# One core, windowed attention and a graph feed-forward: the second stream's output projection with tokens in rows, its bias and residual added in the PSUM bank by TensorE

## Chip, cores and metric

One Trainium2 (trn2) chip, one of its NeuronCores. The metric is the device time of one execution in microseconds (us); smaller is better. Timed executions of the kernel before took 7975.61, 7982.82 and 7992.23 us, median 7982.82.

## What is computed

The input x is 32 images of 32 x 32 tokens with 128 channels. The reference, cut to what matters:

```python
y  = mhsa(windows(layernorm(x)))                      # stream A: 16 windows of 8x8 tokens, 8 heads
ys = roll(unwindows(y), (-4, -4))
ys = mhsa(windows(ys), shift_mask)                    # stream B: the same weights, masked windows
x  = x + roll(unwindows(ys), (4, 4))                  # x2: residual, 1024 tokens x 128 per image
t  = x + ffn(layernorm(x), edge_index)                # graph attention over 524288 + 32768 edges,
                                                      # top 2 of 4 experts, per token
# mhsa: qkv = x @ w_qkv + b_qkv; softmax(q k^T / 4 + mask) @ v; out @ w_o + b_o   (float32)
```

## The kernel before

The kernel has three stages, one after the other: `attention` (both attention passes of all images and, beside them, a sort of the edge keys on VectorE), `edges` (gathers by GpSimd, segment scans, the experts' matmuls) and `combine` (gates, weighted sum, output).

**Order of the attention stage.** Every engine runs its own program over steps n = -2 to 36, each of eight slots j (PAIRS). In a step stream A works on image n (its inputs for n+1 are being made) and stream B on image n-2; from n = 2 to 31 both are active. In each slot TensorE does, in this order (L899 to L918): `scores` of slot j (L849, matmuls L860 and mask matmuls L865), `turn` of slot j-2 (transposes of the exponentials, L879), `weigh` of slot j-3 (L894), then the slot's tasks. VectorE (L1101 to L1125): `less_maximum` (L1096 reduction and L1098 subtraction, both over the PSUM banks of the scores), operations of the sort (L991 to L997), in every second slot `normalised_output` (L1082, L1085), and in fixed slots layer norm statistics (L980) and `residual`. ScalarE: the exponentials (L724), copies of the turned blocks (L731), normalisation (L688), then the evacuation of each task's bank. There is one pair of score banks: `scores` of slot j+1 waits for L1098 of slot j (`s_sub`).

**Tasks and banks.** A task is a name of `SLOT_TASKS` (L356), such as Ap1 (projection of stream A, half 1). Its matmuls go to one of two PSUM banks `misc`, taken strictly in turn over all tasks (L394 to L399); a task waits until the task two places before it has been evacuated (`s_free`). Blocks of sort keys to be transposed (L842, 136 tasks of the steps with both streams) are put behind the slot's tasks and share the two banks. `LAG` says how many steps behind n the image of a task is.

**Stream B's end.** `attended` (L785, ScalarE L613) transposes the attention output to channels in rows and ScalarE writes it with the bias of v into `attT`, 512 tokens per half (two instructions of 128x256). `projected` (L794 to L803) multiplies by `wo`, channels stay in rows: one matmul of 448 and one of 64 columns undo half of the roll. ScalarE adds `b_o` and writes `zrow` (L643, L645). `result` (L805 to L813, tasks CZ0 and CZ1 of slot 6) transposes `zrow` to tokens in rows, four 128x128 blocks per bank. VectorE adds the residual `xres` out of the bank into `x2` (`residual`, L1055 to L1068), signals `s_x2`, and takes the statistics of four tiles in slot 6 and four in slot 7 (L1116 to L1120). SyncE stores x2 (L502); GpSimd turns the statistics into scales (`deviation`, L550); ScalarE normalises x2 in slots 3 and 5 of the next step.

**The sort's plan.** 754 VectorE operations of the sort are spread over the slots by `place_sort` (L184): each slot gets as much as `spare` (L370 to L378) leaves of `SLOT_US` after the slot's other VectorE work. The stage ends when the last sorted part and the last node rows are stored.

## Time and profile before

| | |
|---|---|
| timed executions (3) | 7975.61 / 7982.82 / 7992.23 us |
| the profiled execution | 7985.52 us, span 7983.8 us |
| attention stage | 0 to about 1979 us, a quarter of the span |
| VectorE busy, 585.7 to 1561.7 us | 931.58 of 976.0 us |
| TensorE matmul busy, the same stretch | 907.34 of 976.0 us |
| ScalarE busy, the same stretch | 764.96 of 976.0 us |
| TensorE's granted clock, the same stretch | 1.00 |

A row of instruction groups has the line in the kernel, the engine, the operation, output<-inputs, shapes and count, then the busy time in us and the mean of one in ns, then the idle time before them and what ended it. A float32 matmul appears as two MATMUL records, a float32 transpose or a bf16 matmul as one. A record's duration includes the pipeline's depth; what an instruction costs its engine in a dense stream is the distance between starts.

### The profile page before, as it was taken

Reading aid. Unit: us, or ns where it says so; the run is one execution under the profiler, and the core shown is the slowest. Engines: PE = TensorE matmul, PEld = TensorE weight load, DVE = VectorE, ACT = ScalarE, POOL = GpSimd, SP = SyncE. Lnnn points to the kernel's source line nnn. Section 1 sums busy time; section 2 is a strip of 40 time slices with the busy share of each in tenths; the row PEclk is TensorE's granted clock in tenths of the full one; section 3 lists DMA queues with packets and bytes.
Section 4 is the critical chain, followed back from the end, with each engine's and each line's share of the span. In section 5 each row is a group of like instructions: output and inputs, shape, how many; then the busy total and the mean of one; then the engine's idle time right before and its main releaser. Section 6 shows DMA issues by size and latency. Waiting matters only on the chain. (4 is left out here: it accounts for less than half of the span.)

```text
span 7983.8 us, 104199 instructions
## 1 busy us (share of the span) xinstructions
PE 4192.2 (53%) x31501; PEld 2296.2 (29%) x31501; DVE 5000.1 (63%) x14844; ACT 2129.2 (27%) x3826; POOL 5007.6 (63%) x5600
## 2 busy tenths in 40 slices
PE   6889999997443453453453454454344344345200
PEld 3666666665121121121121122122122122112000
DVE  9999999998444544554554554554554554454378
ACT  4777777774010010010010010010001001001034
POOL 3232323222777777777777777777777777777672
PEclk8999999997565565565565556566556556556555
DMA  1122222222111111111111111111111111111267
GB/s 50 55 59 58 59 59 59 59 58 69 33 33 33 44 33 33 44 33 33 44 33 33 44 33 33 44 32 33 35 41 33 32 44 33 33 44 32 80 216 249
DMA packets 503707, 419.05 MB, mean 52 GB/s; under 512 B 160530, under 2 KB 400194, under 8 KB 502722
## 3 DMA queue, kind: packets, MB, share of 16 engines
q1 hardware_dynamic: 289138, 323.26, 12.3%
q0 software_dynamic: 147552, 56.96, 6.1%
q10 hardware_dynamic: 66560, 33.56, 1.4%
q8 instruction: 187, 3.06, 0.2%
q14 instruction: 270, 2.21, 0.1%
HBM read 203.37 MB, written 176.45 MB: 48 GB/s over the span
## 5 line engine op out<-in xcount | busy, mean ns | idle before, releaser
L1574 POOL DMA_INDIRECT edge_G<-node_rows,edge_src x4352 | 4177.2, 960 | 1326.3 <-issue 1326.3
L1623 PE MATMUL edge_cbank<-edge_ohh,edge_ohl 128*128 128x256 bf16 x4096 | 1417.5, 394 | 2962.6 <-DVE edge_ohh L1391 2871.4
L1623 PEld LDWEIGHTS edge_cbank<-edge_ohh,edge_ohl 128*128 128x128 bf16 x4096 | 427.2, 104 | 3946.3 <-DVE edge_ohh L1391 3773.1
L1391 DVE TENSOR_SCALAR edge_ohh<-edge_iob,edge_dlf 128x256 bf16<-128x256 bf16 x4096 | 1204.1, 300 | 0.1
L1390 DVE TENSOR_SCALAR edge_ohl<-edge_iob,edge_dlf 128x128 bf16<-128x128 bf16 x4096 | 1095.1, 268 | 14.8 <-DVE edge_dlf L1384 13.1
L1599 ACT ACTIVATE edge_hid<-edge_hbank,edge_b1c 128x512 f32<-128x512 f32 x512 | 351.6, 687 | 2508.1 <-PE edge_hbank L1630 2508.1
L1349 DVE COPY edge_O<-edge_O 128x24 f32<-128x24 f32 x64 | 11.9, 186 | 1536.5 <-DMA edge_G<-node_rows,edge_src 1536.5
L557 POOL TENSOR_TENSOR attn_nw<-attn_st 128x8 f32<-128x8 f32 x64 | 84.6, 1321 | 1341.5 <-DVE attn_st L980 1341.5
L1403 DVE TENSOR_TENSOR edge_yo<-edge_ybank,edge_b2r 128x512 f32<-128x512 f32 x256 | 177.1, 692 | 946.6 <-PE edge_ybank L1639 946.6
L1602 ACT ACTIVATE edge_w<-edge_w 128x272 f32<-128x272 f32 x64 | 27.5, 429 | 2413.2 <-DVE edge_w L1363 2413.2
L1630 PE MATMUL edge_hbank<-edge_xt,edge_w 128*128 128x512 f32 x1024 | 590.3, 726 | 0.9 <-ACT edge_hid L1599 0.9
L1639 PE MATMUL edge_ybank<-edge_w,edge_hid 128*128 128x128 f32 x4096 | 474.0, 277 | 54.3 <-ACT edge_hid L1599 54.3
L1639 PEld LDWEIGHTS edge_ybank<-edge_w,edge_hid 128*128 128x128 f32 x4096 | 462.2, 192 | 107.0 <-issue 100.6
L991 DVE TENSOR_TENSOR attn_keys<-attn_keys 128x1024 f32<-128x1024 f32 (+1 forms) x340 | 476.9, 1403 | 6.4 <-DVE attn_keys L996 0.5
L996 DVE TENSOR_TENSOR attn_keys<-attn_keys 128x1024 f32<-128x1024 f32 (+1 forms) x340 | 476.5, 1401 | 0.0
L1096 DVE TENSOR_REDUCE attn_mx<-attn_score 128x16 f32<-128x1024 f32 (+1 forms) x272 | 314.2, 1155 | 46.6 <-PE attn_score L865 26.5
L860 PE MATMUL attn_score<-attn_km,attn_qT 64*64 64x256 f32 x4096 | 292.8, 398 | 92.7 <-DVE attn_S L1098 83.4
L1098 DVE TENSOR_TENSOR attn_S<-attn_score,attn_mx 128x1024 f32<-128x1024 f32 (+1 forms) x272 | 316.0, 1162 | 9.3
L1772 POOL DMA_INDIRECT comb_srow<-state_rows,end_index x256 | 256.9, 1004 | 87.2 <-issue 77.7
L731 ACT ACTIVATE attn_pT<-attn_turn 128x1024 f32<-128x1024 f32 (+1 forms) x272 | 264.7, 973 | 167.0 <-PE attn_turn L879 165.7
L894 PE MATMUL attn_out<-attn_vx,attn_pT 128*64 128x34 f32 x8192 | 296.8, 227 | 12.1 <-DVE attn_att L1085 12.1
L1630 PEld LDWEIGHTS edge_hbank<-edge_xt,edge_w 128*128 128x128 f32 x1024 | 202.3, 229 | 342.6 <-ACT edge_hid L1599 254.2
(244 smaller groups left out, 6448.1 us busy)
## 6 DMA issues: line engine op xcount, KB each, us to landing
edge_G<-node_rows,edge_src POOLq DMA_INDIRECT x4352, 2.3
expert_out<-edge_yo SPq DMA_DIRECT2D x64, 1024.0 KB
comb_ye<-expert_out SPq DMA_DIRECT2D x32, 2048.0 KB, 11.7
state_rows<-edge_O SPq DMA_DIRECT2D x64, 816.0 KB, 3.7
attn_km<-attn_kT SPq DMA_DIRECT2D x1024, 32.0 KB, 2.0
attn_xin<-in_x SPq DMA_DIRECT2D x32, 512.0 KB, 4.3
attn_xres<-in_x SPq DMA_DIRECT2D x32, 512.0 KB, 5.1
x_rows<-attn_x SPq DMA_DIRECT2D x32, 512.0 KB, 3.1
```

The source lines that it names most:

```text
L894: last = pe.matmul(out_bank[e * WTOK:(e + 1) * WTOK, j % OUT_SLOTS, c:c + VW], pT[j % 2][:, st, g, e * WTOK:(e + 1) * WTOK], vx[st][:, 2 * ...
L991: return dve.tensor_tensor(out, a, b, ALU.min)
L996: return dve.tensor_tensor(out, a, b, ALU.max)
L1096: dve.tensor_reduce(top, scores, AX_X, ALU.max).then_inc(s_mx, 1)
L1098: dve.tensor_tensor(S[j % RING_S][:, :, lo:hi, :, :].rearrange("p a s h k -> p a (s h) k"), scores, top.unsqueeze(3).to_broadcast([P, 2, ( ...
L1390: dve.tensor_scalar(ohl[:, t % RING, :], iob[:, 0:P], dlf[:, 0, t:t + 1], None, ALU.is_equal)
L1391: dve.tensor_scalar(ohh[:, t % RING, :], iob[:, :], dlf[:, 1, t:t + 1], None, ALU.is_equal).then_inc(s_oh, 1)
L1574: pool.indirect_dma_start(G[b][:, t, :], None, node_rows, bass.IndirectOffsetOnAxis(ap=src[b][:, t:t + 1], axis=0)).then_inc(s_g[b][2 * t ...
L1599: act.activation(hid[:, k, :], hbank[k % 2][:, :], ACT.Gelu, bias=b1c[:, k:k + 1]).then_inc(s_ge, 1)
L1623: pe.matmul(cbank[b][:, 0:HI], ohl[:, t % RING, :], ohh[:, t % RING, :], start=(t == 0), stop=(t == HC - 1)).then_inc(s_ohp, 1)
L1630: pe.matmul(hbank[k % 2][:, :], w1[:, k // HB, (k % HB) * P:(k % HB + 1) * P], xt[b][:, :], start=True, stop=True).then_inc(s_l1, 1)
L1639: last = pe.matmul(ybank[t % 2][:, x * P:(x + 1) * P], hid[:, x * HB + h, t * P:(t + 1) * P], w2[:, x, h, :], start=(h == 0), stop=(h == H ...
```

## The change

Only stream B's end changes, and the plan of the sort with it.

- `attended` of stream B writes all 1024 tokens of an image to `attB`, already rolled by four columns: three ScalarE instructions per quarter (192, 32 and 32 columns) instead of one of 256.
- The tasks Bp0 and Bp1 are gone from slots 0 and 4, with their matmuls and with `zrow`.
- `result` (CZ0, CZ1, slot 6) makes the bank by matmuls that accumulate: a bf16 matmul of ones with `osplit` (three rows that hold the bias b_o in three bf16 parts, 512 columns), the identity times `xres` (float32, 512 columns), and four float32 matmuls with a 128x128 block of `attB` as the stationary operand and `wo` (128 columns) as the moving one. TensorE now waits for `s_xres` here.
- ScalarE copies the bank into `x2` (new `result`), waiting for the store, the statistics and the normalisation of the image before.
- VectorE's `residual` is gone, with `s_x2`; all eight tiles of statistics are taken at the end of slot 7, behind the slot's sort operations.
- Ten small VectorE operations and one DMA prepare `osplit` at the start.
- `SLOT_US` goes from 8.05 to 7.8, the other work of slot 6 from 3.2 to 0 and that of slot 7 from 1.8 to 3.0.

The diff, cut to its core:

```diff
-        zrow = sb("zrow", [P, TOKENS])
+        obias = sb("obias", [P, P])
+        orest = sb("orest", [P, P])
+        oparts = [sb(f"oparts{i}", [P, P], BF16) for i in range(3)]
+        osplit = sb("osplit", [P, TILES // 2, P], BF16)
+        all_ones = sb("all_ones", [P, P], BF16)
...
-        attT = [sb(f"attT{s}", [P, BANK]) for s in range(2)]
+        attA = sb("attA", [P, BANK])
+        attB = sb("attB", [P, SIDE, SIDE])
...
-        SLOT_TASKS = [["Ap0", "Bp0", "Av0", "Bv0"],
+        SLOT_TASKS = [["Ap0", "Av0", "Bv0"],
...
-                      ["Ap1", "Bp1"],
+                      ["Ap1"],
...
-        SLOT_US = 8.05
+        SLOT_US = 7.8
...
-            busy += {4: 3.6, 6: 3.2, 7: 1.8}.get(j, 0.0)
+            busy += {4: 3.6, 7: 3.0}.get(j, 0.0)
...
+            sp.dma_start(obias[:, :], b_o.rearrange("(o d) -> o d", o=1).to_broadcast([P, P])).then_inc(s_w, 16)
...
-                        sp.wait_ge(s_x2, m)
+
+                        wait_full(sp, "CZ0", m - 1)
+                        wait_full(sp, "CZ1", m - 1)
...
-                    sp.wait_ge(s_x2, m + 1)
+                    wait_free(sp, "CZ0", m)
+                    wait_free(sp, "CZ1", m)
...
+                if task[0] == "B" and m > 0:
+                    wait_full(act, "CZ0", m - 1)
+                    wait_full(act, "CZ1", m - 1)
                 for a in range(2):
                     c = slice(a * 256, (a + 1) * 256)
-                    last = act.activation(dst[:, c].rearrange("p (h b c) -> p h b c", h=WIN, b=WGRID),
-                                          t[:, c].rearrange("p (b h c) -> p h b c", b=WGRID, h=WIN), ACT.Identity, bias=bias[:, 2:3])
+                    src = t[:, c].rearrange("p (b h c) -> p h b c", b=WGRID, h=WIN)
+                    if task[0] == "A":
+                        last = act.activation(attA[:, c].rearrange("p (h b c) -> p h b c", h=WIN, b=WGRID), src, ACT.Identity,
+                                              bias=bias[:, 2:3])
+                        continue
+                    rows = attB[:, (2 * h + a) * WIN:(2 * h + a + 1) * WIN, :]
+                    whole = SIDE - WIN
+                    act.activation(rows[:, :, SHIFT:SHIFT + whole].rearrange("p h (b c) -> p h b c", c=WIN), src[:, :, 0:WGRID - 1, :],
+                                   ACT.Identity, bias=bias[:, 2:3])
+                    act.activation(rows[:, :, SHIFT + whole:SIDE], src[:, :, WGRID - 1, 0:SHIFT], ACT.Identity, bias=bias[:, 2:3])
+                    last = act.activation(rows[:, :, 0:SHIFT], src[:, :, WGRID - 1, SHIFT:WIN], ACT.Identity, bias=bias[:, 2:3])
...
-                else:
-                    if m > 0:
-                        wait_full(act, "CZ0", m - 1)
-                        wait_full(act, "CZ1", m - 1)
-                    first = (h * TOKENS // 2 + SHIFT * SIDE)
-                    size = min(BANK, TOKENS - first)
-                    last = act.activation(zrow[:, first:first + size], t[:, 0:size], ACT.Identity, bias=bias[:, 3:4])
-                    if size < BANK:
-                        last = act.activation(zrow[:, 0:BANK - size], t[:, size:], ACT.Identity, bias=bias[:, 3:4])
...
+            def result(n, task):
+
+                m, i = n - LAG[task], int(task[2])
+                t, free = take(n, task)
+                if m > 0:
+
+                    act.wait_ge(s_x2st, 16 * m)
+                    act.wait_ge(s_moment[1], m)
+                    act.wait_ge(s_tn, 2 * m)
+                act.activation(x2[:, 4 * i:4 * i + 4, :].rearrange("p j d -> p (j d)"), t[:, :], ACT.Copy).then_inc(free, 1)
...
             def result(n, task):
-                i = int(task[2])
+                m, i = n - LAG[task], int(task[2])
                 t = take(n, task)
                 for h in range(2):
-                    wait_free(pe, f"Bp{h}", n - LAG[task])
+                    wait_free(pe, f"Bo{h}", m)
+                pe.wait_ge(s_xres, 16 * m + 16)
+                pe.matmul(t[:, :], all_ones[:, :], osplit[:, :, :].rearrange("p j d -> p (j d)"), start=True, stop=False)
+                pe.matmul(t[:, :], ident[:, :], xres[:, 4 * i:4 * i + 4, :].rearrange("p j d -> p (j d)"), start=False, stop=False)
                 for k in range(4):
-                    c = (4 * i + k) * P
-                    last = pe.transpose(t[:, k * P:(k + 1) * P], zrow[:, c:c + P], ident[:, :])
+
+                    r = (4 * i + k - 1) % TILES * SHIFT
+                    last = pe.matmul(t[:, k * P:(k + 1) * P], attB[:, r:r + SHIFT, :].rearrange("p r c -> p (r c)"), wo[:, :],
+                                     start=False, stop=k == 3)
...
+            dve.memset(osplit[:, :, :], 0.0)
+            dve.memset(all_ones[:, :], 1.0)
+            link(dve.tensor_copy(oparts[0][:, :], obias[:, :]))
+            link(dve.tensor_tensor(orest[:, :], obias[:, :], oparts[0][:, :], ALU.subtract))
+            link(dve.tensor_copy(oparts[1][:, :], orest[:, :]))
+            link(dve.tensor_tensor(orest[:, :], orest[:, :], oparts[1][:, :], ALU.subtract))
+            link(dve.tensor_copy(oparts[2][:, :], orest[:, :]))
+            for i in range(3):
+                row = slice(32 * i, 32 * i + 1)
+                last = dve.tensor_copy(osplit[row, :, :], oparts[i][row, :].unsqueeze(1).to_broadcast([1, TILES // 2, P]))
+            link(last)
...
-            def residual(n):
-                m = n - LAG["CZ0"]
-                dve.wait_ge(s_xres, 16 * m + 16)
-                if m > 0:
-                    dve.wait_ge(s_x2st, 16 * m)
-                    dve.wait_ge(s_tn, 2 * m)
-                for i in range(2):
-                    b, k = where(n, f"CZ{i}")
-                    dve.wait_ge(s_full[b], k)
-                    z = misc[b][:, :].rearrange("p (j d) -> p j d", d=P)
-                    dve.tensor_tensor(x2[:, 4 * i:4 * i + 4, :], z, xres[:, 4 * i:4 * i + 4, :], ALU.add).then_inc(s_free[b], 1)
-                for i in range(2):
-                    wait_free(dve, f"CZ{i}", m)
-                dve.sem_inc(s_x2, 1)
...
-                    if j == 6 and active("CZ0", n):
-                        residual(n)
-                        statistics(1, x2, range(0, TILES // 2), n - LAG["CZ0"])
-                    if j == 7 and active("CZ0", n):
-                        statistics(1, x2, range(TILES // 2, TILES), n - LAG["CZ0"])
...
+                    if j == 7 and active("CZ0", n):
+                        for i in range(2):
+                            wait_free(dve, f"CZ{i}", n - LAG["CZ0"])
+                        statistics(1, x2, range(TILES), n - LAG["CZ0"])
```

## Rows read from the trace of the kernel before

**Rows 1.** The page: busy time of every engine
```profile
PE 4192.2 (53%) x31501; PEld 2296.2 (29%) x31501; DVE 5000.1 (63%) x14844; ACT 2129.2 (27%) x3826; POOL 5007.6 (63%) x5600
```

**Rows 2.** Stretches: start:end, us; busy PE, PEld, DVE, ACT, POOL; clock, DMA, GB/s
```profile
191.50:585.70 394.20, 345.76 (x4694) 242.48 (x4695) 386.83 (x389) 286.02 (x496) 116.07 (x205) 0.99 0.21 58
585.70:1561.70 976.00, 907.34 (x11993) 638.88 (x11989) 931.58 (x1120) 764.96 (x1389) 272.49 (x507) 1.00 0.21 58
1561.70:1791.10 229.40, 208.74 (x2792) 147.07 (x2788) 218.63 (x251) 174.92 (x308) 60.93 (x107) 1.00 0.21 57
```

**Rows 3.** Waits, 191.5 to 585.7 us: us in total, times, longest us
```profile
PE attn_score L860 <- DVE attn_S L1098: 28.9, 23, 3.2
```

**Rows 4.** Waits, 585.7 to 1561.7 us
```profile
DVE attn_mx L1096 <- PE attn_score L865: 14.0, 8, 6.3
...
DVE attn_mx L1096 <- PE attn_score L860: 11.5, 13, 1.7
...
PE attn_score L860 <- DVE attn_S L1098: 3.5, 8, 0.6
```

**Rows 5.** Waits, 1561.7 to 1791.1 us
```profile
PE attn_score L860 <- DVE attn_S L1098: 8.5, 8, 1.8
```

**Rows 6.** Timeline of TensorE in one step: start us, us, then the group
```profile
1026.35 0.97 PE L801 MATMUL attn_misc<-attn_attT,attn_wo 128*128 128x448 f32 x2
...
1027.42 1.09 PE L860 MATMUL attn_score<-attn_km,attn_qT 64*64 64x256 f32 x16
...
1034.76 1.09 PE L860 MATMUL attn_score<-attn_km,attn_qT 64*64 64x256 f32 x16
...
1037.97 1.98 PE L771 MATMUL attn_misc<-attn_ywin,attn_wqkv 128*128 128x512 f32 x4
1039.88 0.66 PE L812 MATMUL attn_misc<-attn_ident,attn_zrow 128*128 128x128 f32 x4
...
1041.32 1.09 PE L860 MATMUL attn_score<-attn_km,attn_qT 64*64 64x256 f32 x16
...
1052.91 0.97 PE L801 MATMUL attn_misc<-attn_attT,attn_wo 128*128 128x448 f32 x2
...
1054.15 1.15 PE L781 MATMUL attn_misc<-attn_wqkv,attn_wmaj 128*64 128x64 f32 x32
```

**Rows 7.** Timeline of all engines, slots 6 and 7 of the same step
```profile
1041.02 1.29 DVE L1065 TENSOR_TENSOR attn_x<-attn_misc,attn_xres 128x512 f32<-128x512 f32 x2 [0.35 <-issue]
...
1042.45 0.88 DVE L980 BATCH_NORM_STATS2 attn_st<-attn_x 128x6 f32<-128x128 f32 x4
...
1045.23 1.57 ACT L619 ACTIVATE attn_attT<-attn_misc,attn_bias 128x256 f32<-128x256 f32 x4 [0.62 <-PE attn_misc L791]
...
1046.85 0.42 PEld L820 LDWEIGHTS attn_misc<-attn_ident,attn_normed 128*128 128x128 f32 x4 [0.31 <-ACT attn_attT L619]
```

**Rows 8.** Timeline of TensorE: float32 128x128 with fresh weights, edges stage; mask matmuls
```profile
2123.56 7.41 PE L1639 MATMUL edge_ybank<-edge_w,edge_hid 128*128 128x128 f32 x64 [0.78 <-ACT edge_hid L1599]
...
1000.02 0.28 PE L865 MATMUL attn_score<-attn_masks,attn_ones 64*64 64x256 bf16 x2
1000.23 1.09 PE L879 MATMUL attn_turn<-attn_ident,attn_S 128*128 128x128 f32 x8
```

**Rows 9.** Groups of the attention stage by shape: two sizes of ScalarE's instructions
```profile
L643 ACT ACTIVATE attn_zrow<-attn_misc,attn_bias 128x512 f32<-128x512 f32 x32 | 22.0, 687 | 1.7 <-PE attn_misc L803 1.7
...
L645 ACT ACTIVATE attn_zrow<-attn_misc,attn_bias 128x128 f32<-128x128 f32 x32 | 11.5, 359 | 0.0
```

**Rows 10.** Timeline of the first 60 us
```profile
6.00 1.63 DVE L936 CAST attn_ones<-attn_ident 128x128 bf16<-128x128 f32 x1
...
8.75 6.96 POOL L540 MEMSET attn_km<- 128x4096 f32 x2
...
18.38 4.43 DVE L959 TENSOR_TENSOR attn_keys<-attn_keys 128x4096 int32<-128x4096 int32 x1 [7.78 <-DMA attn_keys<-in_L_ffn_edge_index]
...
59.57 1.13 PE L860 MATMUL attn_score<-attn_km,attn_qT 64*64 64x256 f32 x8 [12.64 <-DVE attn_S L1098]
```

More of the change, by code:

```diff
@@ L247 @@
 KM_DONE = 16 * HEADS
-SETUP = 8
+SETUP = 14
 OUT_SLOTS = 2
@@ L363, in attention @@
                       ["Ao0", "Bo0", "CT0", "CT1"]]
-        LAG = {"Ap0": 1, "Bp0": 3, "Av0": 0, "Bv0": 2, "Ak1": 0, "Bk1": 2, "Aq1": 0, "Bq1": 2, "Av1": 0, "Bv1": 2,
-               "FT0": -1, "FT1": -1, "Ao1": 1, "Bo1": 3, "Ap1": 1, "Bp1": 3, "Ak0": -1, "Aq0": -1, "CH0": 5,
+        LAG = {"Ap0": 1, "Av0": 0, "Bv0": 2, "Ak1": 0, "Bk1": 2, "Aq1": 0, "Bq1": 2, "Av1": 0, "Bv1": 2,
+               "FT0": -1, "FT1": -1, "Ao1": 1, "Bo1": 3, "Ap1": 1, "Ak0": -1, "Aq0": -1, "CH0": 5,
                "Bk0": 1, "Bq0": 1, "CZ0": 3, "CZ1": 3, "Ao0": 0, "Bo0": 2, "CT0": 4, "CT1": 4, "A": 0, "B": 2}
         FIRST_STEP, LAST_STEP = -2, IMAGES + 5
-        SLOT_US = 8.05
+        SLOT_US = 7.8
         def spare(slot):
@@ L580, in _ @@
         def _(act):
-            act.wait_ge(s_w, 16 * 7)
+            act.wait_ge(s_w, 16 * 8)
             act.wait_ge(s_c, 13)
@@ L613, in attended @@
             def attended(n, task):
[L615 removed]
+                m, h = n - LAG[task], int(task[2])
                 t, free = take(n, task)
+                if task[0] == "B" and m > 0:
+                    wait_full(act, "CZ0", m - 1)
+                    wait_full(act, "CZ1", m - 1)
                 for a in range(2):
                     c = slice(a * 256, (a + 1) * 256)
[L619 to L620 removed]
+                    src = t[:, c].rearrange("p (b h c) -> p h b c", b=WGRID, h=WIN)
[9 more added lines that the diff above has]
+                    last = act.activation(rows[:, :, 0:SHIFT], src[:, :, WGRID - 1, SHIFT:WIN], ACT.Identity, bias=bias[:, 2:3])
                 last.then_inc(free, 1)
@@ L627, in projected @@
                 t, free = take(n, task)
-                if task[0] == "A":
-                    if m > 1:
-                        wait_full(act, "Bv1", m - 2)
-                    for a, first, r, rows in (((2 * h - 1) % WGRID, WIN - SHIFT, 0, SHIFT), (2 * h, 0, SHIFT, WIN),
-                                              (2 * h + 1, 0, SHIFT + WIN, SHIFT)):
-                        out = ywin[m % 2][:, a, :, :].rearrange("p b (h c) -> p h b c", h=WIN)[:, first:first + rows]
-                        src = t[:, r * SIDE:(r + rows) * SIDE].rearrange("p (h b c) -> p h b c", h=rows, b=WGRID)
-                        last = act.activation(out, src, ACT.Identity, bias=bias[:, 3:4])
-                else:
-                    if m > 0:
-                        wait_full(act, "CZ0", m - 1)
-                        wait_full(act, "CZ1", m - 1)
-                    first = (h * TOKENS // 2 + SHIFT * SIDE)
-                    size = min(BANK, TOKENS - first)
-                    last = act.activation(zrow[:, first:first + size], t[:, 0:size], ACT.Identity, bias=bias[:, 3:4])
-                    if size < BANK:
-                        last = act.activation(zrow[:, 0:BANK - size], t[:, size:], ACT.Identity, bias=bias[:, 3:4])
-                last.then_inc(free, 1)
+                if m > 1:
+                    wait_full(act, "Bv1", m - 2)
+                for a, first, r, rows in (((2 * h - 1) % WGRID, WIN - SHIFT, 0, SHIFT), (2 * h, 0, SHIFT, WIN),
+                                          (2 * h + 1, 0, SHIFT + WIN, SHIFT)):
+                    out = ywin[m % 2][:, a, :, :].rearrange("p b (h c) -> p h b c", h=WIN)[:, first:first + rows]
+                    src = t[:, r * SIDE:(r + rows) * SIDE].rearrange("p (h b c) -> p h b c", h=rows, b=WGRID)
+                    last = act.activation(out, src, ACT.Identity, bias=bias[:, 3:4])
+                last.then_inc(free, 1)
+            def result(n, task):
[6 more added lines that the diff above has]
+                act.activation(x2[:, 4 * i:4 * i + 4, :].rearrange("p j d -> p (j d)"), t[:, :], ACT.Copy).then_inc(free, 1)
             def tokens(n, task):
@@ L713, in _ @@
             KINDS = {"Aq": queries_or_keys, "Ak": queries_or_keys, "Bq": queries_or_keys, "Bk": queries_or_keys,
-                     "Av": values, "Bv": values, "Ao": attended, "Bo": attended, "Ap": projected, "Bp": projected,
-                     "CT": tokens, "FT": image, "CH": features}
+                     "Av": values, "Bv": values, "Ao": attended, "Bo": attended, "Ap": projected,
+                     "CZ": result, "CT": tokens, "FT": image, "CH": features}
             for n in steps:
@@ L748, in _ @@
         def _(pe):
-            pe.wait_ge(s_w, 16 * 7)
+            pe.wait_ge(s_w, 16 * 8)
             pe.wait_ge(s_c, 13)
@@ L845, in _ @@
             KINDS = {"Aq": queries_or_keys, "Ak": queries_or_keys, "Bq": queries_or_keys, "Bk": queries_or_keys,
-                     "Av": values, "Bv": values, "Ao": attended, "Bo": attended, "Ap": projected, "Bp": projected,
+                     "Av": values, "Bv": values, "Ao": attended, "Bo": attended, "Ap": projected,
                      "CT": tiles, "FT": tiles, "CZ": result, "CH": graph_features}
```

16 lines of the change are left out of this document (6 added, 10 removed).

## Prediction, written before the changed kernel ran

> **What bounds the kernel now.** I read the busy times of the page first: no engine is full over the whole span, 63% at most [rows 1], so the limit changes from stage to stage. The change touches neither the edges stage nor the last one; only the first quarter matters, and I cut it into stretches. In the 28 steps whose boundaries fall at 191.5, 585.7, 1561.7 and 1791.1 us (7, 17 and 4 steps) TensorE has the full clock and two engines are nearly full: VectorE for 98%, 95% and 95% of the time, TensorE for 88%, 93% and 91% [rows 2]. A step takes 56.3, 57.4 and 57.4 us there. Busy time alone doesn't say which of the two sets the pace; the waits do. In the first stretch TensorE waits for VectorE's release of the scores 28.9 us, 4.1 us a step [rows 3]: VectorE paces. In the long middle stretch it is turned round: TensorE waits for the scores' release 3.5 us in all 17 steps, while VectorE waits 14.0 + 11.5 us for scores [rows 4]. TensorE now also transposes sort keys, and it paces. In the last stretch TensorE waits 8.5 us for VectorE, 2.1 a step [rows 5]: mixed.
>
> The change takes work from VectorE and gives work to TensorE and ScalarE. So it should help where VectorE paces and cost where TensorE does, and there are 17 steps of the second kind to about 12 of the first.
>
> **TensorE, per step.** *Removed:* in slot 4 the projection of Bp1 goes, 1026.35 to 1027.42: 1.07 us. In slot 0 that of Bp0, 1052.91 to 1054.15, is 1.24 us with a wait in it; the next but one task still waits for the same evacuation, so I count 1.0. In slot 6 the two tasks of transposes go from 1039.88 to 1041.32, 1.44 us [rows 6]. Together 3.51 us.
> *Added in slot 6, per bank:* (a) the identity times 512 float32 columns. Two such matmuls (four records) take 1037.97 to 1039.88, so one takes 0.96 us [rows 6]. (b) Four float32 matmuls, each with a fresh 128x128 block and 128 moving columns. The same form runs in the edges stage: 64 records in 7.41 us are 0.116 a record, 0.23 a matmul, 0.93 for four [rows 8]. (c) The bf16 matmul of ones, 512 columns. The nearest row is the mask matmul of 256 bf16 columns, 0.21 us from start to start [rows 8]. Lower bound that 0.21, upper bound the 0.48 of a float32 record of the same 512 columns [rows 6]; I take 0.30, near the row of its own type. The sum is 2.19 a bank, 4.38 for two (bounds 4.20 and 4.74).
> The Trainium skill ("TensorE: Matmul & The Clock Gate", section "Wait — 56ns, not 53.3ns?") has such a matmul start 215.7 ns before the next; with that the two banks would be estimated 0.17 us cheaper. No row here shows this form.
> Net matmul time: 4.38 - 3.51 = +0.87 us a step.
>
> **What moves on ScalarE and comes back to TensorE.** `attended` of stream B becomes three instructions per quarter. Four instructions of 256 columns take 1.57 us, 0.39 each from start to start [rows 7]. From the 512- and 128-column rows (687 and 359 ns) an instruction costs about 0.85 ns a column above a fixed part of 0.25 us [rows 9]. As 256 columns come to 0.47 that way against 0.39 from start to start, 0.08 overlaps with the next instruction. So 192 + 32 + 32 columns take 0.33 + 0.20 + 0.20 = 0.73 instead of 0.39, and a task takes 0.68 longer to free its bank, with rounding 0.7. In slot 7 that delay lies on TensorE's path: CT1 needs the bank of Bo0, and already now its weight load sits 0.31 us until the last `attended` instruction ends [rows 7]. There it costs +0.7 (bounds 0, if ScalarE's other work gave the time back, and 1.0). In slot 3 only steps with two sort blocks behind Bo1 feel it; the plan has about 6 such pairs in 30 steps, +0.15 a step. ScalarE's total grows by 1.4 us, and two copies of 512 columns replace three of `zrow` (about 1.6 us): it was busy for 78% of the middle stretch [rows 2], and stays off the path. Its wait for CZ1 in slot 6 holds up the exponentials of slot 7 behind it, which TensorE needs only a slot later.
> TensorE together: +0.87 + 0.7 + 0.15 = about +1.7 us a step (bounds +0.6 and +2.4).
>
> **VectorE, per step.** The two additions take 1041.02 to 1042.45, 1.43 us with their signal [rows 7]. The statistics only move. The sort has the same 754 operations. I worked the plan's own formula through with both sets of numbers: `SLOT_US` loses 0.25 in each of eight slots, the other work of slots 6 and 7 loses 2.0, so a step keeps its share, the last operation stays in the same slot (297), and what moves is 57 operations into slot 6 (25 to 82 in the 30 two-stream steps), taken from slot 7 (60 to 25) and slot 2 (102 to 84). That follows the work: slot 6 becomes TensorE's longest. It lasts from 1034.76 to 1041.32 now, 6.6 us [rows 6], and 6.6 - 1.44 + 4.38 = 9.5 then. VectorE: -1.43 a step.
>
> **The sum.** *Middle 17 steps:* TensorE paces, +1.7; of the 0.2 us that it waits for VectorE a step, most goes. 17 x 1.55 = +26. *First 8 two-stream steps (n = 2 to 9):* TensorE without its waits takes 56.3 - 4.1 = 52.2, with the change 53.9; VectorE 56.3 - 1.4 = 54.9 still paces: I take -1.2 a step, a little lost to slots that don't match, -10. *Steps 27 to 30:* TensorE 57.4 - 2.1 + 1.7 = 57.0, -0.4 a step, -2. *Steps 31 to 36:* stream A runs out and the sort on VectorE sets the end: about -2. *The start:* the ten preparing operations. A cast beside GpSimd's memset took 1.63 us, and GpSimd memsets until 15.7 us [rows 10]; the new casts may wait till then, and the first image's statistics with them. But the keys land only at 18.38, and TensorE later waits 12.64 us for VectorE [rows 10], so of this delay I count +1 (bounds 0 and +5). SyncE's longer waits (the load of xres behind CZ, the store behind ScalarE's copy) have a slot or more of room. In all +26 - 10 - 2 - 2 + 1 = **+13 us**. Against the profiled execution's 7985.5 (span 7983.8 and 1.7 around it) that is 7998.5; it stood 2.7 above the median of the runs, so I predict 7996.
>
> **The rivals.**
> *VectorE is the bound everywhere.* It is busy 95% of the middle stretch, TensorE's weight loads only 638.88 of 976.0 us [rows 2]. Then TensorE's extra hides in its slack and each of 32 images gives back 1.43 us: -46, 7937. The waits speak against it [rows 4]; for it speaks that VectorE's own work, 931.58 / 17 = 54.8 us, is only 2.6 short of a step. The Trainium skill says so outright: "Perfetto Trace Analysis", section "Identifying the Most-Contended Engine", takes VectorE's occupancy as it stands and tells not to judge TensorE by matmul busy time but by weight-load share and useful work. By that rule TensorE has room here; rows 4, a wait for its scores, do not agree. I give it 0.25.
> *Slot 6 is too long (ends slower).* With one pair of score banks neither engine can run more than part of a slot ahead. TensorE's slot 6 becomes 9.5 us where the mean slot is 57.4 / 8 = 7.2, while slots 4 and 0, relieved by 1 us each, may be those in which VectorE paces. Then the relief is worth nothing, and a step pays the 2.9 us of slot 6 and the 0.7 of slot 7, less VectorE's 1.43: +2.2 over 28 steps, +62, 8045. It decides when VectorE's waits for scores come once in nearly every step and last 2 us or more, instead of 25.5 us in 17 steps [rows 4]. I give it 0.25.
> *It cancels out:* the relief and the load meet and the time stays within 5 us, about 7983. That is my forecast's lower half and no case of its own.
>
> **How the numbers follow.** The forecast has 0.5; its own range, from +0.6 to +2.4 a step on TensorE over 17 steps and the start's bounds, is 7977 to 8012. A measurement here can tell about 0.2%, 16 us, from no change. Of the forecast's half, 0.37 lies within and 0.13 above; of VectorE's rival 0.24 below and 0.01 within; of slot 6's 0.24 above and 0.01 within. So faster 0.24, same 0.39, slower 0.37. The range leaves out the outer half of either rival: 7945 to 8035.
>
> **What would show it.** Right: in the changed kernel's middle steps TensorE's waits for VectorE stay near nothing, VectorE's waits for scores grow to 2 us a step or more, TensorE's slot 6 tasks take 4.2 to 4.7 us, CT1's wait on ScalarE grows to about 1 us, and the seven steps of the first stretch are shorter than 56.3. Wrong: if the middle steps fall to about 55.5 with TensorE waiting for VectorE (the first rival), or if every step grows by over 2 us with VectorE idle in slot 7 and TensorE idle before slots 1 or 5 (the second).

## The result, and the profile after

The changed kernel takes **8036.95 us** (median of 4 runs, 8029.45 to 8042.13), the kernel before 7981.06 in the same comparison: a ratio of **1.0067, 95% interval 1.0055 to 1.0079**. It is slower by 56 us. 7996 was forecast, and 8036.95 lies just outside the range of 7945 to 8035; by the ratio's interval the two cannot be told apart (1.0055 of the 7982.82 us on which the forecast stood is 8026.7). The rival "slot 6 is too long" had 8045. The profiled execution took 8042.13 us, span 8040.4; against the span of before that is +56.6 us, and the accounts below are made between these two profiles.

The page gives the same picture as [rows 1]: no engine is full, TensorE has 34 us more, VectorE 41 less.

```profile
PE 4226.6 (53%) x31661; PEld 2337.6 (29%) x31693; DVE 4959.2 (62%) x14790; ACT 2151.6 (27%) x4050; POOL 4921.1 (61%) x5600
```

A step begins with the first score subtraction of its slot 0 (L1119, before L1098). The windows between the same steps as in [rows 2] (3 to 9, 10 to 26, 27 to 30; columns as there):

```profile
206.80:607.80 401.00, 359.83 (x4764) 255.09 (x4771) 377.82 (x375) 291.71 (x546) 100.23 (x210) 0.96 0.20 57
607.80:1612.20 1004.40, 920.13 (x12058) 656.50 (x12071) 913.75 (x1086) 775.68 (x1508) 228.64 (x506) 0.99 0.20 57
1612.20:1855.00 242.80, 215.08 (x2805) 153.90 (x2806) 209.94 (x243) 177.12 (x333) 41.43 (x106) 0.97 0.19 53
```

From these starts and the last subtraction (1926.05 us before, 1995.31 after) comes the account. The forecast for the first steps was -10 over eight; steps 3 to 9 are seven of them, and the eighth lies in the start.

| part | forecast | measured |
|---|---|---|
| start, to step 3 (191.5 to 206.8) | -1 (+1, and -2 for step 2) | +15.3 |
| steps 3 to 9 | -8 | +6.8 |
| steps 10 to 26 | +26 | +28.4 |
| steps 27 to 30 | -2 | +13.4 |
| step 31 to the last subtraction | -2 | +5.4 |
| what follows it (6057.7 to 6045.1) | 0 | -12.7 |

The middle came out as forecast; the start and both stretches in which VectorE should have gained did not. The **waits** say why. Steps 3 to 9 (before [rows 3]):

```profile
PE attn_score L884 <- DVE attn_S L1119: 24.9, 15, 2.6
...
DVE attn_mx L1117 <- PE attn_score L884: 12.3, 6, 3.9
DVE attn_mx L1117 <- PE attn_score L889: 7.5, 6, 3.3
```

Both engines now wait for each other: VectorE 19.8 us in seven steps for scores, and TensorE still 24.9 (28.9 before) for the bank's release. In steps 27 to 30 TensorE's wait is 15.6 us (8.5 in [rows 5]) and VectorE's two waits for scores are 15.6 us each. The middle steps (before [rows 4]):

```profile
DVE attn_mx L1117 <- PE attn_score L889: 39.6, 30, 5.1
DVE attn_mx L1117 <- PE attn_score L884: 38.2, 25, 2.8
...
PE attn_misc L866 <- ACT attn_ywin L654: 11.8, 12, 1.3
PE attn_misc L844 <- ACT attn_attB L640: 11.5, 17, 0.7
...
PE attn_score L884 <- DVE attn_S L1119: 8.2, 13, 1.1
...
PE attn_misc L866 <- ACT attn_attB L640: 3.4, 5, 0.7
```

VectorE waits 77.8 us for scores, 4.6 a step, where it was 1.5. The line with `ywin` is new and was not forecast. Slots 6 and 7 in the **timeline** of one middle step show where VectorE's waits begin (compare [rows 6, 7]):

```profile
1013.75 1.02 PE L831 MATMUL attn_misc<-attn_xres,attn_ident 128*128 128x512 f32 x2
1014.61 1.05 PE L835 MATMUL attn_misc<-attn_wo,attn_attB 128*128 128x128 f32 x8
1015.50 0.38 PE L830 MATMUL attn_misc<-attn_osplit,attn_all_ones 128*128 128x512 bf16 x1
1015.72 1.02 PE L831 MATMUL attn_misc<-attn_xres,attn_ident 128*128 128x512 f32 x2
1016.58 1.05 PE L835 MATMUL attn_misc<-attn_wo,attn_attB 128*128 128x128 f32 x8
1017.56 1.09 PE L884 MATMUL attn_score<-attn_km,attn_qT 64*64 64x256 f32 x16
...
1023.69 0.66 PE L844 MATMUL attn_misc<-attn_ident,attn_normed 128*128 128x128 f32 x4 [0.68 <-ACT attn_attB L640]
```

```profile
1018.81 1.22 DVE L1117 TENSOR_REDUCE attn_mx<-attn_score 128x16 f32<-128x1024 f32 x1 [1.23 <-PE attn_score L889]
...
1025.44 1.22 DVE L1117 TENSOR_REDUCE attn_mx<-attn_score 128x16 f32<-128x1024 f32 x1 [1.47 <-PE attn_score L884]
```

The second bank takes 1015.50 to 1017.56, 2.06 us (2.19 forecast). The slot from VectorE's subtraction 6 to subtraction 7 lasts on average 7.07 us before and 8.54 after in steps 3 to 9, 7.17 and 8.59 in the middle, 6.90 and 9.64 in steps 27 to 30; slot 4, relieved of Bp1, is 5.72 and 5.86, 6.08 and 6.06, 5.94 and 5.39. So slot 4 gave next to nothing back, except in the last four steps, and slot 6 paid. In the middle slot 7 grew as well, from 5.78 to 7.03 us: slots 6 and 7 together took 2.67 us more.

**What TensorE did in slot 4, and its clock.** With Bp1 gone TensorE has little to do in slot 4 and then waits for VectorE's release. In steps 3 to 9 and 27 to 30 it waits 2.5 us or more there nine times, up to 3.95; before, a single wait for that release was that long (3.25, in step 9). In seven of the nine the granted clock fell during the wait or right behind it. Step 27 shows what follows (TensorE):

```profile
1638.54 1.02 PE L820 MATMUL attn_misc<-attn_attA,attn_wo 128*128 128x448 f32 x2
1639.39 0.33 PE L821 MATMUL attn_misc<-attn_attA,attn_wo 128*128 128x64 f32 x2
1643.68 1.13 PE L884 MATMUL attn_score<-attn_km,attn_qT 64*64 64x256 f32 x16 [3.95 <-DVE attn_S L1119]
...
1644.95 1.97 PE L903 MATMUL attn_turn<-attn_ident,attn_S 128*128 128x128 f32 x8
...
1663.85 1.09 PE L903 MATMUL attn_turn<-attn_ident,attn_S 128*128 128x128 f32 x8
```

```profile
1638.00:1644.60 6.60, 2.65 (x42) 1.79 (x40) 6.50 (x7) 3.86 (x7) 0.00 (x0) 1.00 0.20 59
1644.60:1648.00 3.40, 3.40 (x36) 2.72 (x32) 3.37 (x11) 1.16 (x3) 1.37 (x7) 0.50 0.02 5
```

TensorE was busy for 2.65 of the 6.60 us from 1638.00 to 1644.60 (windows as above). Then the granted clock is 0.50 for 3.4 us, the lower of its two levels (1.2 GHz), and the same eight transposes take 1.97 us instead of 1.09. The granted clock is 0.96, 0.99 and 0.97 in the three windows above, where [rows 2] have 0.99, 1.00 and 1.00: some 28 us at the lower level in steps 3 to 9 (10 before) and 14 in steps 27 to 30 (none before). Part of what TensorE's busy time grew by there, 14.1 and 6.3 us, is the clock and not the new matmuls.

**The start** (before [rows 10]), VectorE and then GpSimd:

```profile
11.12 1.20 DVE L973 CAST attn_oparts<-attn_obias 128x128 bf16<-128x128 f32 x1
12.35 0.29 DVE L974 TENSOR_TENSOR attn_orest<-attn_obias,attn_oparts 128x128 f32<-128x128 f32 x1
12.68 3.17 DVE L975 CAST attn_oparts<-attn_orest 128x128 bf16<-128x128 f32 x1
...
17.95 1.65 DVE L1016 BATCH_NORM_STATS2 attn_st<-attn_xin 128x6 f32<-128x128 f32 x8
20.32 4.43 DVE L995 TENSOR_TENSOR attn_keys<-attn_keys 128x4096 int32<-128x4096 int32 x1 [0.73 <-DMA attn_keys<-in_L_ffn_edge_index]
```

```profile
8.72 7.04 POOL L548 MEMSET attn_km<- 128x4096 f32 x2
19.75 0.21 POOL L565 TENSOR_TENSOR attn_nw<-attn_st 128x8 f32<-128x8 f32 x1 [3.98 <-DVE attn_st L1016]
...
20.37 4.43 POOL L568 TENSOR_SCALAR attn_nw<-attn_nw 128x8 f32<-128x8 f32 x1
...
34.69 7.76 POOL L575 TENSOR_TENSOR attn_nw<-attn_nw 128x8 f32<-128x8 f32 x1
...
46.05 1.06 POOL L579 TENSOR_TENSOR attn_nw<-attn_nw 128x8 f32<-128x8 f32 x1
```

The second cast ends when GpSimd's fill of `km` ends (15.76 us); the statistics come at 17.95 us, where they came at 8.96 before and GpSimd, busy with the fill, took them up at 15.67. GpSimd's chain of 15 tiny operations then starts at 19.75 instead of 15.67, which is not much. But now it meets VectorE's passes over the keys: one operation of 8 columns lasts 4.43 us, just as long as the 4.43 of L995 beside it, another 7.76. The scales are ready at 47.1 us; before, the last operation of that chain (L571) began at 25.73. The first score subtraction comes at 69.4 instead of 58.8.
The Trainium skill ("SBUF — State Buffer", section "Who interferes with whom") says that VectorE's casts can run in a mode that takes a pair of ports shared with GpSimd, that whoever issues first then blocks the other for its whole instruction, and that a VectorE operation with two inputs in SBUF contends with a GpSimd operation that reads SBUF. Both fences agree: 15.85 beside 15.76, 4.43 beside 4.43.

### The profile page after: what moved, and what is told of

Read it like the earlier page. It is cut to its first block and busy times, and to the rows that moved or that the text cites. A ratio compares the mean times of both kernels' runs of the same rounds, so it can differ in the third digit from the quotient of the medians.

```text
span 8040.4 us, 104846 instructions
## 1 busy us (share of the span) xinstructions
PE 4226.6 (53%) x31661; PEld 2337.6 (29%) x31693; DVE 4959.2 (62%) x14790; ACT 2151.6 (27%) x4050; POOL 4921.1 (61%) x5600
## 5 line engine op out<-in xcount | busy, mean ns | idle before, releaser
L565 POOL TENSOR_TENSOR attn_nw<-attn_st 128x8 f32<-128x8 f32 x64 | 42.4, 662 | 1486.4 <-DVE attn_st L1016 1486.4
L1119 DVE TENSOR_TENSOR attn_S<-attn_score,attn_mx 128x1024 f32<-128x1024 f32 (+1 forms) x272 | 315.9, 1162 | 9.3
```

The lines of the kernel that those rows point to most:

```text
L1119: dve.tensor_tensor(S[j % RING_S][:, :, lo:hi, :, :].rearrange("p a s h k -> p a (s h) k"), scores, top.unsqueeze(3).to_broadcast([P, 2, ( ...
```

## The experiments

The attention stage repeats closely, so beside the ratio I give the time of its last score subtraction: 1926.05 us before, 1995.31 after. Unless said otherwise each kernel is the changed one with one edit.

**1. The preparing operations later.**

```diff
             dve.wait_ge(s_w, 16 * 8)
-            dve.memset(osplit[:, :, :], 0.0)
-            dve.memset(all_ones[:, :], 1.0)
-            link(dve.tensor_copy(oparts[0][:, :], obias[:, :]))
...
+                    if n == 0 and j == 2:
+                        prepare_bias()
```

> The kernel after, with the ten preparing operations of VectorE (casts and differences for the bias and the identity) moved out of the start into a step of the stage with one stream, and the load of the bias issued last, on a semaphore of its own. Theory: the start slipped by 15 us (step 3 began at 191.5 us before and at 206.8 us after) because these operations wait at the start and push the first statistics back, and all steps after it inherit that: step 3 begins near 192 us again and the time falls by 15 us, to about 8022. Rival: a slip of the start is taken up later, by sort operations that fill idle slots: step 3 begins earlier, and the time stays within 3 us of 8037.

8014.66 us, ratio 1.0057 (1.0040 to 1.0073), last subtraction 1978.32, -17.0. The first subtraction is back at 58.6 us, step 3 begins at 197.8 (-9.0), and the rest of the gain falls in the steps behind it. The same two casts now take 0.16 and 0.23 us instead of 1.20 and 3.17. So the preparing operations did delay the first subtraction. But step 3 begins only 9.0 us earlier, not the 15 expected; in the kernels with the sort's new plan it comes 135 to 139 us after the first subtraction, in those with the old plan 132 to 135. Of the gain behind step 3, 4.4 us in steps 3 to 9 and 3.5 in the middle came with a higher granted clock (0.98 and 1.00 instead of 0.96 and 0.99). The whole time fell by some 8 us by the ratio, less than the stage: see run 12.

**2. The old plan of the sort.**

```diff
-        SLOT_US = 7.8
+        SLOT_US = 8.05
-            busy += {4: 3.6, 7: 3.0}.get(j, 0.0)
+            busy += {4: 3.6, 6: 3.2, 7: 1.8}.get(j, 0.0)
```

> The kernel after, with the slot lengths of the plan before (8.05 us a slot, 3.6 in slot 4, 3.2 in slot 6, 1.8 in slot 7), so that the sort operations lie in the slots as before. Theory: the new time is TensorE's net load and the length of slot 6, not where the sort operations lie: the time stays within 10 us of 8037. Rival: the plan, remade for other slot lengths, is at fault: 20 us or more faster, 8017 or below.

8026.25 us, ratio 1.0068 (1.0052 to 1.0085), last subtraction 1993.75. Where the sort operations lie is not the cause of the loss, though it shifts it: the start is 6.1 us shorter and steps 3 to 9 are 6.3 us longer (407.3).

**3. One instruction of ScalarE in place of three.** It leaves out the roll by four columns.

```diff
-                    act.activation(rows[:, :, SHIFT + whole:SIDE], src[:, :, WGRID - 1, 0:SHIFT], ACT.Identity, bias=bias[:, 2:3])
-                    last = act.activation(rows[:, :, 0:SHIFT], src[:, :, WGRID - 1, SHIFT:WIN], ACT.Identity, bias=bias[:, 2:3])
+                    last = act.activation(rows.rearrange("p h (b c) -> p h b c", c=WIN), src, ACT.Identity, bias=bias[:, 2:3])
```

> The kernel after, with one instruction of ScalarE in place of three for each quarter of stream B's attention (it leaves out the roll by four columns). Theory: the longer evacuation holds the transposes of slot 7 back by 0.7 us a step (the wait of 0.68 us in the timeline), 28 steps by 0.7: 20 us faster, about 8017. Rival: ScalarE's evacuation is the main cost of the change: 40 us or more faster, 7997 or below.

8002.34 us, ratio 1.0040 (1.0026 to 1.0054), last subtraction 1972.42, -22.9, nearly all of it in the middle (1004.4 to 984.5). Forecast -20. Steps 27 to 30 did not gain (244.3 us, at a granted clock of 0.95).

**4. No residual.** It leaves out the second stream's residual.

```diff
-                pe.matmul(t[:, :], ident[:, :], xres[:, 4 * i:4 * i + 4, :].rearrange("p j d -> p (j d)"), start=False, stop=False)
```

> The kernel after without the product of the identity and the stream's input (it leaves out the residual of the second stream). Theory: slot 6 holds too much work of TensorE (8.6 us after, 7.1 before), and this takes 2 by 0.86 us out of it; 28 steps by 1.6 us: 45 us faster, about 7992, with slot 6 near 7.2 us and VectorE's wait for scores behind it gone. Rival: ScalarE's chain, not TensorE's columns, sets the end of slot 6 and 7: 10 us faster at most, 8027 or above.

7973.24 us, ratio 1.0003 (0.9994 to 1.0013), last subtraction 1945.64, -49.7. The middle steps fell by 1.85 us each (59.08 to 57.24) for 1.72 us of matmuls (twice 1013.75 to 1014.61 in the timeline above). TensorE's columns in slot 6 are paid for in full there, although its weight loads fill only 656.50 of the 1004.40 us. The prediction's first rival does not hold for this stretch. Nor does the rule of the Trainium skill beside it ("Perfetto Trace Analysis", section "Identifying the Most-Contended Engine"), as far as it goes by the weight loads' share; the useful work was not worked out. In steps 27 to 30 only 2.2 of the 13.4 us came back (240.6), although slot 6 lost 1.72 us of matmuls in each: the wait of 3.96 us in slot 4 stayed, and the granted clock was 0.95. Slot 6's length alone does not explain those steps.

**5. The two result banks in two slots.** Same columns of TensorE, other place. The edit also issues the load of the residual at the top of the step and lets ScalarE's first copy wait for one normalisation fewer; in the changed kernel neither TensorE's product nor ScalarE's copy is ever seen waiting for these.

```diff
-                      ["Ap1"],
+                      ["Ap1", "CZ0"],
-                      ["Bk0", "Bq0", "CZ0", "CZ1"],
+                      ["Bk0", "Bq0", "CZ1"],
...
-                    act.wait_ge(s_tn, 2 * m)
+                    act.wait_ge(s_tn, 2 * m + i - 1)
```

> The kernel after, with its two result banks apart, the first in slot 4 and the second in slot 6 (the loads of the residual go out at the top of the step). TensorE's columns stay the same. Theory A, TensorE's columns and its waits for ScalarE set the middle steps, and slot 6's length costs only where VectorE is late (steps 3 to 9 and 27 to 30): the last subtraction of the attention stage comes 10 to 20 us earlier than 1995.3 us, and the middle steps stay within 0.3 us of 59.08. Theory B, slot 6's length costs in every step: 35 us or more earlier, middle steps 1 us or more shorter. Theory C, only the total counts: within 8 us.

7972.95 us, ratio 1.0008 (0.9998 to 1.0017), last subtraction 1943.18, **-52.1**. My theory A fell; B, the second rival's mechanism, is right in size. Steps 3 to 9 take 385.3 us (401.0 after, 394.2 before), 27 to 30 take 230.2 (242.8), the middle 983.9 (1004.4), as the windows show:

```profile
205.20:590.50 385.30, 351.81 (x4771) 249.31 (x4770) 377.19 (x375) 291.27 (x546) 101.68 (x205) 0.99 0.21 58
590.50:1574.40 983.90, 917.34 (x12078) 653.31 (x12075) 913.89 (x1087) 775.64 (x1508) 228.83 (x511) 1.00 0.22 58
1574.40:1804.60 230.20, 210.17 (x2808) 149.52 (x2804) 209.57 (x242) 176.55 (x333) 42.40 (x103) 1.00 0.21 56
```

VectorE's busy time is that of the changed kernel within 1 us in each. In the middle steps' waits the line with `ywin` is gone (11.8 us) and the wait for the scores' release shrank from 8.2:

```profile
PE attn_score L884 <- DVE attn_S L1119: 1.3, 3, 0.5
```

Together 18.7 of the 20.5 us. Between VectorE's subtractions the gain stands in slot 6 (8.59 to 7.29), not in slot 4 (6.06 to 6.08). So two things are mixed here: slot 6's length, and the empty place in slot 4. The empty place also carries the clock: with CZ0 in slot 4 no wait of TensorE for VectorE in steps 3 to 30 reaches 2.5 us, and the granted clock is 0.99, 1.00 and 1.00 again. The same matmuls then keep TensorE busy for 8.0, 2.8 and 4.9 us less in the three stretches; from that I estimate the clock's part of the gain at some 16 us at most. Run 11 tries slot 4's order alone.

**6. The preparing operations in the kernel before.** Their results are not used.

```diff
             dve.wait_ge(s_w, 16 * 8)
+            dve.memset(osplit[:, :, :], 0.0)
+            dve.memset(all_ones[:, :], 1.0)
+            link(dve.tensor_copy(oparts[0][:, :], obias[:, :]))
...
```

> The kernel before with nothing but the preparing operations at the start (the load of the bias, two fills and eight casts and differences of VectorE; their results are not used). Theory: they alone cost what the first run took back by moving them, so the last subtraction comes 14 to 18 us later than 1926.1 us. Rival: the start slips for another reason (the new order of slots), and these operations cost 0 to 4 us. A second reading: the stage after the last subtraction took 6057.7 us in the profiled kernel before and 6030 to 6032 us in all runs of the first set; if that is the chip and not the kernel, it is 6030 to 6035 us here, if it is the kernel, 6040 us or more.

Ratio 0.9999 (0.9989 to 1.0008), but last subtraction 1933.89. In the stage they cost 7.8 us, half of what I gave them: step 3 begins at 201.7 (+10.2), and 2.4 us are made good later. GpSimd's chain runs here from 20.28 to 47.41 us, as in the changed kernel, so it is these operations that move it. In the whole time it doesn't show, since the stage behind it took only 6027.7 us.

**7. A version between the two:** tokens in rows and the bias in the bank, but VectorE adds the residual as before.

```diff
-                pe.matmul(t[:, :], ident[:, :], xres[:, 4 * i:4 * i + 4, :].rearrange("p j d -> p (j d)"), start=False, stop=False)
+                    dve.tensor_tensor(x2[:, 4 * i:4 * i + 4, :], z, xres[:, 4 * i:4 * i + 4, :], ALU.add).then_inc(s_free[b], 1)
```

> A version between the two: tokens in rows and the bias in TensorE's bank as after, but VectorE adds the residual as before (no product with the identity, no copy by ScalarE), the preparing operations in a step of the stage with one stream, the plan's slot lengths as before. Theory: TensorE's columns per step are then 1.72 us fewer than after, the wait of 0.68 us for ScalarE's three instructions stays, so the middle steps take about 57.2 us (before 57.4), and the last subtraction comes at 1920 to 1935 us, level with before within 0.1%. Rival, VectorE's adding binds again: middle steps 58 us or more, last subtraction after 1945 us.

7982.1 us, ratio 1.0015 (1.0005 to 1.0025), last subtraction 1947.57, as the rival said. The middle steps take 57.70 us, between the theory's 57.2 and the rival's 58; steps 3 to 9 take 57.57, more than before or after, since VectorE stands in slot 6 until TensorE has filled a bank (8.76 us between its subtractions 6 and 7).

**8. The same with four instructions of ScalarE for a half instead of six** (the two small ones of both quarters in one).

```diff
-                    act.activation(rows[:, :, SHIFT + whole:SIDE], src[:, :, WGRID - 1, 0:SHIFT], ACT.Identity, bias=bias[:, 2:3])
+                act.activation(rows[:, :, :, SHIFT + whole:SIDE], src[:, :, WGRID - 1, :, 0:SHIFT], ACT.Identity, bias=bias[:, 2:3])
```

> The version between the two, with stream B's attention taken out of its bank in four instructions of ScalarE for a half instead of six (the two small ones of both quarters in one each). Theory: the wait of 0.68 us in slot 7 shrinks by the duration of two small instructions, 0.4 us or so a step, 28 steps: 8 to 12 us less than the version with six, the last subtraction at 1910 to 1925 us, and the whole 0.1 to 0.2% faster than before. Rival: a larger instruction costs as much as two small ones, or the wait isn't on the path: within 3 us of the version with six.

7970.65 us, ratio 1.0008 (0.9998 to 1.0017), last subtraction 1936.26, -11.3 against run 7, as forecast; but it stays behind the 1910 to 1925 us that were expected, and the kernel is not faster than before. TensorE's wait in slot 7 fell from 0.68 to 0.38 us.

**9. Three edits at once:** those of runs 1 and 5 and the four instructions.

```diff
+                    if n == 0 and j == 2:
+                        prepare_bias()
...
-                      ["Ap1"],
+                      ["Ap1", "CZ0"],
...
+                act.activation(rows[:, :, :, SHIFT + whole:SIDE], src[:, :, WGRID - 1, :, 0:SHIFT], ACT.Identity, bias=bias[:, 2:3])
```

> The kernel after with three edits at once: the two result banks apart (slots 4 and 6), the preparing operations in a step of the stage with one stream, and stream B's attention taken out of its bank in four instructions of ScalarE instead of six. Theory: the parts add up. The banks apart gave 52 us of the attention stage (last subtraction 1995.3 to 1943.2 us), the preparing operations 17 us, the four instructions 11 us in the version between the two (1947.6 to 1936.3 us): the last subtraction comes at 1910 to 1922 us, and the whole is 0 to 0.2% faster than before. Rival: the three take away the same waits, and VectorE binds instead: last subtraction at 1930 us or later.

**7957.39 us, ratio 0.9982 (0.9972 to 0.9992)**, some 14 us below before; against the change that is some 0.8%, from the two ratios. The last subtraction comes at 1925.64 us, between the theory (up to 1922) and the rival (from 1930); the sum of the parts would have been 1915. That is level with the kernel before (1926.05 and, in run 12, 1924.59). So the loss of the change is made good, but no gain of the stage over before is shown: the 14 us lie behind the stage, in the part whose length run 12 cannot explain.

**10. The same with VectorE's addition:** run 8 with the banks apart, the first added in slot 4, and the plan's slot lengths fitted to that.

```diff
-                    if j == 6 and active("CZ0", n):
-                        residual(n)
+                    if j in (4, 6) and active("CZ0", n):
+                        residual(n, (j - 4) // 2)
```

> The version between the two (VectorE adds the residual, four instructions of ScalarE) with the banks apart as well: the first result and its addition in slot 4, the second in slot 6, statistics in slots 5 and 7. Theory: TensorE's columns are then 1.1 us a step fewer than before, slot 4 keeps a bank between the projection and the turned sort keys, and slot 6 is short: middle steps 55.8 to 56.6 us (before 57.4), steps 3 to 9 near 56.3 as before, last subtraction at 1900 to 1915 us, the whole 0.1 to 0.3% faster than before. Rival, VectorE's additions and waits bind: middle steps 57 us or more and the last subtraction at 1925 us or later.

8016.47 us, ratio 1.0057 (1.0040 to 1.0074), last subtraction 1970.09. It lost 34 us against run 8: 41 in the middle (59.76 us a step), of which the other stretches gave some back. The first line of TensorE's waits there:

```profile
PE attn_misc L857 <- DVE attn_x L1079: 41.2, 14, 4.3
```

The transposes of the sort keys want the bank that VectorE has not yet emptied in slot 4. There its addition comes behind half of the slot's sort operations and `normalised_output`, and everything that TensorE has queued behind that bank stands for up to 4.3 us.

**11. Only the order in slot 4.** The banks stay together in slot 6.

```diff
+            return turned + own if j == 4 and active("A", n) and active("B", n) else own + turned
```

> The kernel after, with one order changed: in slot 4 of the steps with two streams the turned sort keys come ahead of the projection, so that their transposes do not stand behind the bank that ScalarE is still emptying for the projection. The result banks stay together in slot 6. Theory: that wait (12 times 1.0 us in the middle steps, 0 in steps 3 to 9) is one part of what moving the banks apart gave in the middle steps, the shorter slot 6 is the other: middle steps 0.5 to 0.8 us shorter than 59.08, steps 3 to 9 and 27 to 30 unchanged within 3 us, last subtraction 9 to 14 us earlier than 1995.3 us. Rival, only slot 6's length counts: within 3 us of 1995.3 us.

Ratio 1.0057 (1.0040 to 1.0074), last subtraction 1978.14. The middle took 998.4 us, -0.35 a step, less than I expected (run 1, without this edit, has 1000.9), and the wait did not go; it changed its name:

```profile
PE attn_misc L821 <- ACT attn_keys L704: 11.8, 12, 1.5
```

Now the projection waits for the bank of the keys, the same 12 times and 11.8 us. Whichever comes first, the second waits for a bank that ScalarE is still emptying, when no task stands in between; removing Bp1 took it away, and CZ0 in run 5 put one back. Of the other 11 us of this run most fell in the start (201.0) and in steps 3 to 9 (396.6), which the edit doesn't touch: in the kernels with the preparing operations at the start the first subtraction comes anywhere from 66.1 to 69.7 us, and the steps behind it follow. The clock goes with it: steps 3 to 9 take 396.6 us at a granted clock of 0.98 here and in run 1, 401.0 at 0.96 in the changed kernel. So some 5 to 10 us of any comparison with 1995.31 may be that. Against run 1's stretches, run 5 gained 41 us in the 28 steps instead of 49. How much of it belongs to slot 6's length and how much to the empty slot 4, no run separates.

**12. The kernel before, again.**

> The kernel before, unchanged, profiled on this chip. Its last subtraction should come at 1926.1 us within 1 us if the attention stage runs the same each time. The stage behind it took 6057.7 us in the profile of before and 6028 to 6033 us in the eight runs so far: if that is the chip, it is 6028 to 6033 us here and the whole is nearer to 7960 us; if it belongs to the kernel, 6038 us or more. In both cases the ratio to before is 1.000 within 0.001.

Ratio 1.0002, last subtraction 1924.59, within 1.5 us of the first. Behind it 6044.6 us passed (6057.7 in the first profile). In ten of the other kernels it was 6028 to 6036 us, 6045.1 in the changed kernel's profile and 6046.6 in run 10. The difference lies in the 4352 gathers of GpSimd: from the first to the last 5488.0 us here, 5471.2 in run 6, 5502.3 in the first profile, with the same median of 944 ns each. Neither chip nor change sorts these numbers, and what makes them differ stays open; both profiles of the kernel before are among the four long ones, which flatters every whole time that is set against it. It bounds what the whole time can say here to some 15 us, and of the 69 us that the stage lost only 56 are seen in it.

## Why the prediction was off

- **TensorE's net matmul time, +0.87 a step:** somewhat too large. A bank took 2.06 us against 2.19, so the term is 4.12 - 3.51 = +0.61. Busy time in the middle grew by 12.8 us in 17 steps, 0.75, but at a lower clock; run 1, at 1.00, has 915.4, +0.47 a step. The matmul of ones starts 0.22 us before the next, not 0.30. The Trainium skill's 215.7 ns ("TensorE: Matmul & The Clock Gate", section "Wait — 56ns, not 53.3ns?") agrees.
- **ScalarE's three instructions, +0.7 in slot 7 and +0.15 in slot 3:** right. TensorE's waits for `attended` of both streams grew from 11.8 us (below) to 25.2, 0.79 a step. Run 3 gave 22.9 us back in all.

```profile
PE attn_misc L820 <- ACT attn_attT L619: 8.4, 17, 0.5
PE attn_misc L842 <- ACT attn_attT L619: 3.4, 9, 0.4
```

- **The middle, +26:** right in sum (+28.4), with a term missing and one too small. The wait behind the projection in slot 4 (11.8 us) had been counted as a pure gain of 1.07 us; TensorE's wait for VectorE grew from 3.5 to 8.2 instead of going. Against them stand waits for ScalarE that shrank, such as that of L791, 10.5 to 8.0. So the sum owes part of its fit to errors that met.
- **Steps 3 to 9 and 27 to 30, -1.2 and -0.4 a step: the step that failed.** I set the sum of TensorE's work in a step against the sum of VectorE's and took the larger. With one pair of score banks the comparison holds slot by slot, and slot 6 got 2.7 us more of TensorE's work (4.12 less 1.44), while slots 4 and 0, relieved of 2 us, gave back 0.2 together in steps 3 to 9 (8.12 + 5.72 to 7.81 + 5.86). VectorE set their pace, so TensorE's relief there became waiting, and the clock, a term that the prediction put at nothing, fell to 0.96 and 0.97 on average. The prediction has this as its second rival and names the sign that decides: in the middle VectorE's waits for scores came in every step, 4.6 us together, if only 1.4 each. That the sum was right in itself run 5 shows: with the banks apart steps 3 to 9 gained 1.27 us a step on before, where 1.2 had been forecast, at a granted clock of 0.99 as before.
- **The start, +1: failed.** The prediction saw that the casts might wait for the memset, and put the delay under TensorE's later wait of 12.64 us. But the chain behind the statistics runs on GpSimd, not on VectorE, and 4 us of delay moved it beside the passes over the keys, where it took 27 us instead of some 12. It cost the stage 7.8 us by run 6; run 1's 17.0 are not all due to it, since some 5 to 10 us of such a comparison vary by themselves. Of the start's +15.3 run 6 shows 10.2; run 2, with the sort's old plan, had 6.1 less.
- **The plan of the sort, nothing:** right in sum (run 2).
- **Step 31 to the last subtraction, -2:** it was +5.4 (134.9 to 140.3 us). Run 2, with the old plan, has 136.6; no run takes the rest apart.
- **The rival's own size, 8045:** near, but its price of +2.2 in all 28 steps was not what happened: +0.97, +1.67 and +3.3 a step in the three stretches, and the start made up the rest, so that its total came near is partly luck.

## What to carry to other kernels

Where two engines hand one pair of banks to and fro, compare them slot by slot, and put added work where the slot is short: here the same matmuls cost 41 to 52 us less in another place. Look also at the slots that you relieve: if the other engine sets their pace, the relief becomes waiting, and here the lower clock came with seven of nine such waits. Before removing a small task from a ring of two banks, look at what then stands next to what; it may have been the cover for an evacuation. And judge work moved to the start by what it pushes the rest against.

## What was not expected of the hardware

A GpSimd operation on 8 columns took 0.20 us by itself and 4.43 or 7.76 us beside VectorE's passes over the keys; a VectorE cast of 128 columns took 0.16 us by itself and 1.20 or 3.17 beside GpSimd's memset. And the same 4352 gathers, with one median of 944 ns (947 in two runs), took 5471 to 5502 us from first to last.
